# Writing out the handover from the feed-forward phase to the graph phase of a three-phase Trainium2 kernel

## What is computed

```python
x1 = x + g_msa * attention(modulate(layernorm(x)))             # 16 heads of 64
x2 = x1 + g_mlp * (gelu(modulate(layernorm(x1)) @ W1 + b1) @ W2 + b2)
# graph attention, on x2
self_feat = concat(x2, q) @ W_self.T + b_self     # q is zeroed for rows whose sum is 0
for d in range(2):                                # two directions of the mask
    qh = self_feat @ Wq[d].T + bq[d]; kh = self_feat[:, :20] @ Wk[d].T + bk[d]
    aff = where(cond > 0, qh . kh / sqrt(8), NEG) + label_bias       # 16 heads of 8
    output += softmax(aff) @ self_feat[:, :20] @ Wout[d] + bout[d]
out = x2 + relu(self_feat + output)
```

## Time and profile before

| | |
|---|---|
| three runs | 664.35, 660.92, 662.35 us |
| the profiled execution | 664.79 us |
| its span, first to last instruction | 663.2 us |
| mean granted TensorE clock | 0.982 of full speed |
| TensorE busy | 634.5 us (96%) |
| VectorE, ScalarE, GpSimd busy | 507.8, 478.0, 303.5 us |

### The profile page before, as it was taken

The page is one execution under the profiler, slowest core; times in us unless marked ns, Lnnn a source line. Parts: engine busy times, 40 slices in busy tenths (PEclk is TensorE's granted clock), DMA queues, the critical chain, the costliest instruction groups (busy, mean ns, idle before and its releaser), DMA issues.

```text
span 663.2 us, 16947 instructions
## 1 busy us (share of the span) xinstructions
PE 634.5 (96%) x5432; PEld 548.0 (83%) x5432; DVE 507.8 (77%) x1094; ACT 478.0 (72%) x1707; POOL 303.5 (46%) x341
## 2 busy tenths in 40 slices
PE   7899999999999999999999999899979999999995
PEld 6778889888888888888888887799857888888874
DVE  5888878877887887877877878778546877877774
ACT  4887887888878878878877878488835556555552
POOL 4354354353453444444444445366543465465451
PEclk9999999999999999999999999999978999999997
DMA  8211011011011011011011020233411112212101
GB/s 236 64 36 44 9 49 48 8 43 51 8 43 47 12 43 45 14 43 43 16 43 39 12 61 1 65 95 110 137 48 33 48 49 64 47 53 58 40 25 32
DMA packets 54512, 32.55 MB, mean 49 GB/s; under 512 B 15168, under 2 KB 52304, under 8 KB 54480
## 3 DMA queue, kind: packets, MB, share of 16 engines
q1 hardware_dynamic: 52848, 27.93, 15.5%
q0 software_dynamic: 1632, 4.21, 2.2%
HBM read 25.82 MB, written 6.31 MB: 48 GB/s over the span
## 4 chain that ended last, share of the span: by engine, by line
PE 89%; DVE 6%; SPq 2%; issue 1%; ACT 1%; DMA 0%; POOLq 0%; POOL 0%; DVEq 0%; ACTq 0%
PE banks L601 10%; PE banks L627 9%; PE banks L612 8%; PE banks L572 6%; PE banks L1776 6%; PE banks L1750 6%; PE banks L576 4%; PE banks L573 4%; PE banks L1297 4%; PE banks L585 3%; PE banks L1740 3%; PE banks L1732 3%; PE banks L587 2%; PE banks L648 2%; PE banks L586 2%; PE banks L649 2%
## 5 line engine op out<-in xcount | busy, mean ns | idle before, releaser
L518 POOL TENSOR_TENSOR late_blocks<-late_blocks,p_rsum 128x512 f32<-128x512 f32 x128 | 130.5, 1040 | 209.3 <-DVE p_rsum L934 209.3
L813 ACT ACTIVATE late_blocks<-banks,neg_max 128x128 f32<-128x128 f32 x512 | 182.3, 391 | 2.9 <-DVE neg_max L927 2.9
L813 ACT ACTIVATION_READ_ACCUMULATOR late_blocks<-banks,neg_max 128x1 f32 x512 | 119.0, 232 | 0.0
L791 ACT ACTIVATE wide<-banks 128x512 f32<-128x512 f32 x127 | 78.1, 615 | 38.4 <-PE banks L576 33.6
L947 DVE CAST oT_hi<-banks 128x512 fp32r<-128x512 f32 x60 | 41.5, 692 | 64.4 <-PE banks L627 64.4
L572 PE MATMUL banks<-xT_hi,w_qkv_hi 128*128 128x256 f32 x256 | 82.6, 323 | 2.3 <-ACT wide L791 1.4
L1660 POOL TENSOR_TENSOR late_blocks<-blockmask,g_kT 128x640 f32<-128x640 f32 x32 | 49.5, 1569 | 70.9 <-ACT g_kT L1856 70.9
L927 DVE TENSOR_REDUCE neg_max<-banks 128x8 f32<-128x1024 f32 x64 | 77.2, 1206 | 1.3
L601 PE MATMUL banks<-wide 64*128 64x128 f32 x1024 | 74.4, 285 | 0.0
L576 PE MATMUL banks<-xT_hi,w_qkv_lo 128*128 128x256 f32 x256 | 71.9, 281 | 0.6 <-DVE w_qkv_lo L197 0.6
L573 PE MATMUL banks<-xT_lo,w_qkv_hi 128*128 128x256 f32 x256 | 71.7, 280 | 0.0
(11 more groups left out here) (166 smaller groups left out, 1563.7 us busy)
## 6 DMA issues: line engine op xcount, KB each, us to landing
early<-in_mask SPq DMA_DIRECT2D x16, 220.0 KB
early<-in_mask SPq DMA_DIRECT2D x80, 44.0 KB
x_in<-in_x SPq DMA_DIRECT2D x16, 128.0 KB, 2.1
x_res<-in_x SPq DMA_DIRECT2D x16, 128.0 KB, 2.2
x_scratch<-x SPq DMA_DIRECT2D x16, 128.0 KB, 1.9
f_x_in<-x_scratch SPq DMA_DIRECT2D x16, 128.0 KB, 2.7
f_x_res<-x_scratch POOLq DMA_DIRECT2D x16, 128.0 KB, 2.9
x_scratch<-f_x POOLq DMA_DIRECT2D x16, 128.0 KB, 2.3
```

The lines of the kernel that those rows point to most:

```text
L518: pool.tensor_tensor(p[:, par, heads, :], p[:, par, heads, :], p_rsum[:, par, heads].unsqueeze(2).broadcast_to([128, 4, T]), ALU.mult).the ...
L791: act.activation(dst, proj_ps[k % 2], ACT.Copy).then_inc(proj_saved[k % 2], 1)
L813: act.activation(p[:, par, m, :], s_ps[par][:, e, j, :], ACT.Exp, bias=neg_max[:, par, 4 * e + j:4 * e + j + 1], accum_out=p_sum[:, par, m ...
```

## The change

The first two graph pairs' preparation is placed, instruction by instruction, among the last steps of feed-forward.

- TensorE, ScalarE and VectorE leave the feed-forward loop after step 14 (GpSimd after step 15), and a written-out order follows for each. Steps -2 and -1 of the graph loop are gone.
- `make_bias` goes to the end of VectorE's feed-forward step 10. `turn_sums` is split in two halves, one per bank, each as soon as that bank's gelus are done; `make_turned_bias` waits for each half.
- The table of the exponential is loaded after the gate of pair 14.
- `turns_ps` goes to the low half of bank 2; the turned weights of direction 0 and the keys go to the low half of bank 3. The keys of pair 0 alone go to the high half of bank 2.
- SyncE loads graph pairs 2 and 3 before it waits for all of x2.

```diff
 # feed-forward, TensorE
-            if at(s, PAIRS):
-                output(step_from(s, -1))
-                turn_back(step_from(s, -2))
-                return
...
-        run_bodies(pe, body, start_graph)
+        run_bodies(pe, body, stop=PAIRS - 1)
+
+        begin = graph.parts["tensor_steps"](pe)
+        pe.wait_ge(modulated, PAIRS)
+        begin.turn_x(pair(0))
+        hidden(pair(PAIRS - 1), 0)
+        begin.self_features(pair(0))
+        hidden(pair(PAIRS - 1), 2)
+        turn_back(pair(PAIRS - 3))
+        begin.turn_self(pair(0))
+        pe.wait_ge(gelu_done, (PAIRS - 1) * 4)
+        edges.parts["turn_sums"](pe, 0)
+        pe.wait_ge(gelu_done, PAIRS * 4)
+        edges.parts["turn_sums"](pe, 1)
+        pe.wait_ge(x2_ready, PAIRS - 2)
+        begin.keys(pair(0))
+        begin.queries(pair(0))
+        output(pair(PAIRS - 2))
+        begin.turn_x(pair(1))
+        pe.wait_ge(g.edges_made, 2)
+        begin.affinity(pair(0), 0)
+        begin.self_features(pair(1))
+        output(pair(PAIRS - 1))
+        begin.wait_keys(1)
+        turn_back(pair(PAIRS - 2))
+        begin.turn_self(pair(1))
+        begin.turn_x(pair(2))
+        turn_back(pair(PAIRS - 1))
+        begin.affinity(pair(0), 1)
+        begin.keys(pair(1))
+        begin.queries(pair(1))
+        pe.wait_ge(x2_ready, PAIRS)
 # feed-forward, ScalarE
-            if at(s, PAIRS - 1):
-                load_table(act, ACT.Exp, tables_loaded)
+            if at(s, PAIRS - 2):
+                begin.save_xT(pair(0))
             if more(s, -1):
                 gate(step_from(s, -1))
...
+        gelu(pair(PAIRS - 1), 0)
+        gelu(pair(PAIRS - 1), 2)
+        begin.save_selfT(pair(0))
+        begin.save_k(pair(0))
+        begin.wait_constants()
+        begin.save_q(pair(0))
+        begin.copy_keys(pair(0))
+        gate(pair(PAIRS - 2))
+        begin.save_xT(pair(1))
+        load_table(act, ACT.Exp, tables_loaded)
+        gate(pair(PAIRS - 1))
+        begin.save_selfT(pair(1))
+        begin.weights(pair(0), 0)
+        begin.save_xT(pair(2))
+        begin.save_k(pair(1))
+        begin.save_q(pair(1))
+        begin.copy_keys(pair(1))
 # feed-forward, VectorE
+            if at(s, PAIRS - 6):
+                edges.parts["make_bias"](dve)
...
+        copy_cols(gate_cols, pair(PAIRS - 2), gate_cols_ready)
+        begin.find_nonzero(pair(0))
+        begin.save_self(pair(0))
+        residual(pair(PAIRS - 3))
+        sum_rows(pair(PAIRS - 3))
+        copy_cols(gate_cols, pair(PAIRS - 1), gate_cols_ready)
+        edges.parts["make_turned_bias"](dve)
+        begin.find_nonzero(pair(1))
+        dve.wait_ge(g.edges_made, 2)
+        begin.add_bias(pair(0), 0)
+        begin.save_self(pair(1))
+        begin.row_max(pair(0), 0)
+        begin.shift_scores(pair(0), 0)
+        residual(pair(PAIRS - 2))
+        sum_rows(pair(PAIRS - 2))
+        residual(pair(PAIRS - 1))
+        sum_rows(pair(PAIRS - 1))
+        begin.find_nonzero(pair(2))
 # feed-forward, GpSimd
-        run_bodies(pool, body, None)
+        run_bodies(pool, body, stop=PAIRS)
+        begin = graph.parts["pool_steps"](pool)
+        begin.block_keys(pair(0), 0)
+        begin.block_keys(pair(0), 1)
+        begin.add_output_bias(pair(0))
+        store(pair(PAIRS - 2))
+        store(pair(PAIRS - 1))
+        begin.block_keys(pair(1), 0)
+        begin.block_keys(pair(1), 1)
 # graph phase
-    wT_ps = [g.bank[2][:, 512 * n:512 * n + GCH * T] for n in range(2)]
-    k_ps = g.bank[2][:, GCH * T:GCH * T + 2 * BM]
-    turns_ps = g.bank[3][:, 0:512]
+    wT_ps = [g.bank[3][:, 0:GCH * T], g.bank[2][:, 512:512 + GCH * T]]
+    first_k_ps, next_k_ps = g.bank[2][:, 768:768 + 2 * BM], g.bank[3][:, GCH * T:GCH * T + 2 * BM]
+    turns_ps = g.bank[2][:, 0:512]
...
-        for n in range(-1, 4):
+        for n in range(4):
             body(Step(n // 2, n % 2))
...
             load_res(Step(0, n))
+        sp.wait_ge(g.x2_stored[0], 2 * 16)
+        body(Step(-1, 0))
+        sp.wait_ge(g.x2_stored[1], 2 * 16)
+        body(Step(-1, 1))
         for n in range(2):
             sp.wait_ge(g.x2_stored[n], PAIRS // 2 * 16)
-        body(first_step)
         run_bodies(sp, body)
...
 # turn_x
             zero_wait(pe, selfT_saved, s.n)
+            if at(s, 1):
+                pe.wait_ge(q_saved, 1)
```

More of the change, by code:

```diff
@@ L306, in wait_raw_free, with turn_sums @@
         sp.wait_ge(cells_cast, i)
-    def turn_sums(pe):
+    def turn_sums(pe, which):
         pe.wait_ge(labels_summed, PAIRS)
[L311 to L314, removed]
+        for c in range(ROWCH):
+            last = pe.transpose(g.bank[which][:, c * T:c * T + T],
+                                g.sums[:, which, PAIRS * BM + c * T:PAIRS * BM + c * T + T], g.ident[:])
         last.then_inc(sums_turned, 1)
@@ L1186, in ffn_phase, with run_bodies @@
     tables_loaded = sem("f_tables_loaded")
-    def run_bodies(eng, body, start_graph, start=0):
+    def run_bodies(eng, body, start=0, stop=PAIRS + 2):
         for n in range(start, 4):
@@ L1195, in run_bodies @@
             body(Step(r, 1))
-        for n in range(PAIRS - 6, PAIRS + 2):
-            if n == PAIRS + 1 and start_graph:
-                start_graph(eng)
+        for n in range(PAIRS - 6, stop):
             body(Step(n // 2, n % 2))
+    pair = lambda n: Step(n // 2, n % 2)
     def turn_ps(s):
@@ L1224, in sync @@
         store_last_x1(sp)
-        run_bodies(sp, body, None, start=-1)
+        run_bodies(sp, body, start=-1)
     def gpsimd(pool, part=None):
@@ L1387, in scalar @@
             return
-        run_bodies(act, body, graph.parts["save_first"])
+        begin = graph.parts["scalar_steps"](act)
+        run_bodies(act, body, stop=PAIRS - 1)
+        gelu(pair(PAIRS - 1), 0)
[15 more added lines that the diff above has]
+        begin.copy_keys(pair(1))
     def vector(dve, part=None):
@@ L1722, in keys @@
             for d in range(2):
-                last = pe.matmul(k_ps[:, d * BM:d * BM + BM], g.gqk_w[:, 2 + d, :],
+                last = pe.matmul(k_ps(s)[:, d * BM:d * BM + BM], g.gqk_w[:, 2 + d, :],
                                  selfT[:, :, 0:NG], start=True, stop=True)
@@ L1727, in queries @@
         def queries(s):
-            if more(s, 1):
+            if more(s, 1) and not at(s, 0):
                 pe.wait_ge(xT_saved, s.n + 2)
@@ L1789, in body @@
                 affinity(step_from(s, 1), 0)
-            if second and not at(s, -2):
+            if second:
                 self_features(step_from(s, 2))
@@ L1809, in body, with scalar @@
                 weights_v(s, 1)
[L1811 to L1821, removed]
+        if steps:
+            begin = Kept()
+            begin.turn_x, begin.self_features, begin.turn_self = turn_x, self_features, turn_self
+            begin.keys, begin.queries, begin.affinity = keys, queries, affinity
+            begin.wait_keys = lambda count: pe.wait_ge(k_saved, count)
+            return begin
         run_bodies(pe, body)
-    def scalar(act, first=False):
+    def scalar(act, steps=False):
         def save_xT(s):
@@ L1855, in save_k @@
             for d in range(2):
-                last = act.activation(kT[:, d].rearrange("p b m -> p (b m)"), k_ps[:, d * BM:d * BM + BM],
+                last = act.activation(kT[:, d].rearrange("p b m -> p (b m)"), k_ps(s)[:, d * BM:d * BM + BM],
                                       ACT.Identity, bias=g.gqk_b[:, 2 + d:3 + d])
@@ L1894, in body, with vector @@
                 copy_keys(step_from(s, 2))
[L1896 to L1901, removed]
+        if steps:
+            begin = Kept()
+            begin.save_xT, begin.save_selfT, begin.copy_keys = save_xT, save_selfT, copy_keys
+            begin.save_k, begin.save_q, begin.weights = save_k, save_q, weights
+            begin.wait_constants = lambda: act.wait_ge(consts_set, 1)
+            return begin
         run_bodies(act, body)
-    def vector(dve, first=False):
+    def vector(dve, steps=False):
         def find_nonzero(s):
@@ L1996, in body @@
                 find_nonzero(step_from(s, 3))
[L1998 to L2005, removed]
+        if steps:
+            begin = Kept()
+            begin.save_self, begin.add_bias, begin.row_max = save_self, add_bias, row_max
+            begin.shift_scores = shift_scores
+            begin.find_nonzero = find_nonzero
+            return begin
         run_bodies(dve, body)
```

29 lines of the change are left out of this document (14 added, 15 removed).

## The result

The changed kernel takes 655.32 us (median of 654.63 to 656.03 in four runs) against 663.35 us in the same comparison: ratio 0.988, 95% interval 0.985 to 0.992, 8.0 us less. The forecast was 654.5 us in a range of 652.0 to 659.5 us. The profiled execution took 656.03 us, with a span of 654.5 us, 8.7 us less than the span before. In all that follows, one execution of the kernel before that took 2086.24 us is left out; no trace shows why it was slow.

What follows compares the result with a forecast made beforehand. TensorE bounds the kernel, through the start of the first turned weights. Handover -9.3 us and moved bias table +0.8 us give -8.5 us: 656.3 us against the profiled execution, 653.9 us against the median; 654.5 us named, range 652.0 to 659.5 us.

Steps and rivals of the forecast that it cites:

- What bounds the kernel: TensorE, busy 96% of the span; what matters is when pair 0's first turned weights start, 502.94 us before the change.
- The work of 11.9 us and its waits: Handover from 480.25 us: 11.9 us of TensorE work at full clock plus 1.2 us of waits, 9.3 us saved.
- The date of 494.3 us: Predicted start of the first turned weights in the changed kernel's span, as a sign that the forecast is right.
- the two stores: GpSimd issues them between the blocks of pairs 0 and 1; pair 1's affinity in step 0 then waits some 0.2 us.
- The moved bias table: 1.93 us on VectorE at the end of feed-forward step 10: step 12 starts 1.4 us late, net +0.8 us.
- the bounds of the text: Limits for the moved bias table's cost: 0.3 us if more slack absorbs it, to 1.9 us, the whole table.
- The table load: 1.28 us on ScalarE between output 14 and the last gate, hidden in a 0.9 us wait; no draining counted beside it.
- the sum of 8.5 us: Total predicted gain: -9.3 us in the handover and +0.8 us for the bias table moved into feed-forward.
- the 2.4 us over the median: Profiled execution's surplus over the median run; some may be the slow clock's length, so 654.5 us was named, not 653.9.
- the clock rival: Clock still falls in the 1.0 us idling at 489.5 to 490.5 us: up to 6.8 us lost, 661.3 us; chance 0.10.
- The banks: Swapped bank places make reads collide with TensorE's writes in all 16 pairs; at 0.75 us a pair 665.9 us; chance 0.03.
- the copies under the gelu table: ScalarE's plain copies between gelus reload the table: two loads of 1.28 us, 2.6 us more, 657.1 us; chance 0.03.

Runs made afterwards that it cites:

- filler: Kernel before plus 16 transposes of the identity on TensorE in the handover's idle places, results unread, no wait removed: 658.75 us against 662.26 us, ratio 0.996.
- the banks alone: Kernel before with only the change's bank places for turned inputs, turned weights of direction 0 and keys: 660.97 us against 661.48 us, ratio 0.998.
- both edits: Changed kernel, bias table's three instructions spread over feed-forward steps 10 to 12, pair 0's second affinity ahead of turning graph input 2: 653.72 us, ratio 0.987.
- the third kernel: Changed kernel, bias table spread over steps 10-12, pair 0's second affinity earlier, pair 2's self features before pair 1's affinity: 652.79 us; once more 652.84 us.
- the long idle: Changed kernel with TensorE waiting, ahead of pair 0's second affinity, until the last x2 is in memory: 659.81 us against 655.31 us.
- the three edits and the table back: Changed kernel, bias table back in the handover, pair 0's second affinity before turning graph input 2, pair 2's self features before pair 1's affinity: 652.79 us.

## Why the prediction was right, point by point

- **What bounds the kernel.** Right: the gain is the earlier start of the first turned weights, and the loop behind it is unchanged.
- **The work of 11.9 us and its waits.** The date of 494.3 us becomes 493.9 us if counted from this execution's step 10, which came 0.4 us earlier; 493.76 us was measured. The single waits came where they were named: 1.22 us ahead of graph input 2 (forecast 1.0), 0.30 us at the affinity of pair 1 (0.2), none for the bias tables or for the first block of keys. But the 0.30 us were no cost of the change, as the sum has them: they lie behind the first turned weights, and the old order has them too where the clock holds (0.31 us with filler and with the banks alone). Nor were the two stores their cause: GpSimd was done with these and waited 0.53 us for the saved keys.
- **The moved bias table.** Net +0.7 us for a forecast of +0.8 us, with TensorE idling 1.02 us at the place named. That was net of a DMA wait that the profiled execution before happened to have. Where that wait is absent (14.39 us with filler), the stall costs 1.4 us, within the bounds of the text. The loads of that tile took up to 4.6 us to land in the trace before, and 3.1 us at most in the changed kernel's. So that the net came out at +0.7 us is in part the luck of these two executions.
- **The table load.** The next instruction starts 0.02 us after the load, here too, as the row said. The 1.38 us of draining of the Trainium skill (ScalarE: Activation LUTs, What ACT_TABLE_LOAD costs) doesn't show.
- **The clock.** It held, as forecast, and the idling of 1.2 us didn't bring it down. The affinity matmuls of the handover took 1.17 and 1.08 us up to the next instruction, where they had taken 2.13 us. But the prediction took the slow stretch as a fixed part of the kernel before, and the sum of 8.5 us holds only against an execution that has it in full. Against executions in which the clock held the change is worth 3.7 to 4.0 us (38.46 and 38.70 us from step 10 to the turned weights, against 34.74 us). The rest of the 8.0 us between the medians is the slow stretch that most executions of the kernel before have, worth 3.5 us by the medians of before and filler (662.26 and 658.75 us). None of the ten executions of the changed kernel has a mean granted clock under 0.992, so a stretch as long as before is gone from all of them; a short one can't be told there from the fall near the end. The remark that the 2.4 us over the median might be the slow clock pointed there and should have entered the range: a kernel whose time spreads over 9 us has no single gain. For the profiled execution the sum gave 656.3 us, and 656.03 us was measured. The 1.8 us that were then taken off for the named 654.5 us are in part luck: in the four runs of the changed kernel the two with a mean clock of 0.996 or 0.997 took 654.63 and 654.85 us, and the two with 0.992 or 0.993, like the profiled one with its fall near the end, 655.78 and 656.03 us.
- **The price of the clock rival** was oversized: up to 6.8 us in the text, 2.5 us measured. The slow stretch was half as long (6.8 us), and TensorE worked in only 4.9 us of it, which at half speed loses about 2.5 us. It took an added wait of 3.15 us to bring the clock down; why the stretch was shorter than before is open.
- **The end.** Not forecast: from the first turned weights to the end the changed kernel took 160.74 us in one execution and 158.99 us in another. In the first, with both edits (161.25 us) and in the third kernel once more (160.91 us) the clock fell ahead of the last matmuls. The kernel before has this fall too (160.26 us against 159.0 us with filler and with the banks alone), so it is no cost of the change.
- **The other rivals.** The banks change nothing. No table load was added for the copies under the gelu table: both traces have three loads, one of them at 486.77 us here, and the copy at 479.00 us took its usual 0.38 us.

## What to carry to other kernels

Where one phase hands over to another, count TensorE's work between two dates and compare it with the time that passes; if the clock is low there, first put filler on TensorE, which tells the price of the clock from that of the waits. Take several executions for it, since here the clock fell in some and held in others. Work that is moved into a full pipeline costs what it overruns the slack of its engine, so it should be cut into pieces smaller than the slack, or left where the new order makes that engine wait. When the order of two instructions is free, the one whose operands are ready goes into the wait of the other.

## What the runs showed of the hardware

Nearly the same idling went with different clocks: with 0.54 of 2 us busy at 486 to 488 us (the kernel before) the clock fell to 1.2 GHz for 13.6 us, and with 0.51 of 2 us busy there (the banks alone) it stayed at 2.4 GHz. Within one kernel the mean granted clock ran from 0.976 to 0.998. How long it stayed low differed too: 13.6 us in the kernel before, 6.8 us with the long idle and 3.4 us with the bias table alone moved. The work done in idle places cost nothing by itself: 24.07 us from step 14 to the turned weights with 16 more transposes, and 24.07 us without them where the clock held. The same load of 128 KB in the feed-forward phase landed 2.2 to 4.8 us after its issue, by the traces of the kernel before, the changed one and the one with the three edits and the table back.
